# A macaron layer on one core: shorter filler, one expert's weights on another queue, transposes of the mixed tiles moved

## The reference

```python
x = x + 0.5 * ffn(layernorm(x))
x = x + ssm(layernorm(x))
x = x + 0.5 * ffn(layernorm(x))

def ffn(x):     # 8 experts, top 2 of 8 by sigmoid scores; 2 shared experts
    scores = sigmoid(x @ w_router.T)
    comb = top-2 of scores, divided by their sum
    out  = sum_e comb[:, e] * (silu(x @ wg[e].T) * (x @ wu[e].T)) @ wd[e].T   # inner width 640
    out += sum_j (silu(x @ sg[j].T) * (x @ su[j].T)) @ sd[j].T
def ssm(x):     # selective scan over time, 16 states
    dt = softplus(xproj[:, :256]); B, C = the other 2 x 16 columns of xproj
    h = exp(dt * A) * h + dt * B * x;  y = (h * C).sum(states) + D * x
```

## Time and profile before

| | |
|---|---|
| median of 3 runs | 547.87 us (546.45, 547.87, 549.91) |
| the profiled execution | 546.11 us, of which its span 544.2 |
| TensorE busy | 522.5 us, 96% of the span |
| VectorE busy | 327.8 us |
| GpSimd busy | 230.5 us |
| ScalarE busy | 156.9 us |
| DMA | 67.72 MB, mean 124 GB/s |

### The profile page before, as it was taken

One profiled execution on the slowest core, in us unless ns is written; L12 is line 12 of the kernel. 1 busy time (PEld: TensorE's weight loads), 2 busy tenths in 40 slices (PEclk: granted clock), 3 DMA queues, 4 the chain that ended last, 5 costly groups with the idle time before them and its releaser, 6 DMA issues.

```text
span 544.2 us, 11101 instructions
## 1 busy us (share of the span) xinstructions
PE 522.5 (96%) x4386; PEld 422.4 (78%) x4387; DVE 327.8 (60%) x654; ACT 156.9 (29%) x336; POOL 230.5 (42%) x208
## 2 busy tenths in 40 slices
PE   8999999999979999999979999999997999999996
PEld 7998997458958888447979788964487999954695
DVE  3843526422555999997686399999768232522224
ACT  1111122221117445443202643554421011222210
POOL 1041100322303999995453189999700540000031
PEclk9999999999999999999989999999999999999999
DMA  7986993912204445540321436556100230210012
GB/s 225 398 322 227 394 381 133 316 60 59 70 11 130 114 136 144 152 118 25 105 68 69 118 101 121 133 145 154 34 21 2 98 88 29 78 40 13 20 55 74
DMA packets 41991, 67.72 MB, mean 124 GB/s; under 512 B 5041, under 2 KB 24753, under 8 KB 41937
## 3 DMA queue, kind: packets, MB, share of 16 engines
q1 hardware_dynamic: 29968, 40.75, 25.7%
q10 hardware_dynamic: 8400, 16.12, 8.0%
q0 software_dynamic: 3568, 10.10, 5.5%
HBM read 48.74 MB, written 18.22 MB: 123 GB/s over the span
## 4 chain that ended last, share of the span: by engine, by line
PE 53%; DVE 15%; POOL 14%; issue 10%; DMA 4%; ACT 2%; POOLq 0%; SPq 0%; DVEq 0%; ACTq 0%
PE ps L513 18%; PE ps L528 10%; PE ps L538 10%; POOL region L954 7%; PE ps L551 6%; POOL xnt L968 5%; DVE ps L1035 3%; DMA xg_rows<-region,pos 2%; PE ps L661 2%; PE ps L562 2%; DVE hb L990 2%; PE ps L713 1%; PE ps L683 1%; DMA region<-yg_rows,ypos 1%; PE ps L557 1%
## 5 line engine op out<-in xcount | busy, mean ns | idle before, releaser
L513 PEld LDWEIGHTS ps<-xt,w_gu 128*128 128x128 f32 x1360 | 156.3, 192 | 13.7 <-ACT xt L770 5.6
L513 PE MATMUL ps<-xt,w_gu 128*128 128x128 f32 x1360 | 161.3, 277 | 4.5 <-DVE xres L1005 2.8
L990 DVE SCALAR_TENSOR_TENSOR hb<-hb,ps 128x640 f32<-128x640 f32 x68 | 55.5, 816 | 134.3 <-ACT hb L752 134.0
L538 PE MATMUL ps<-w_dn,hb 128*128 128x256 f32 x520 | 122.1, 383 | 0.0
L538 PEld LDWEIGHTS ps<-w_dn,hb 128*128 128x128 f32 x520 | 96.0, 193 | 11.2
L752 ACT ACTIVATE hb<-ps 128x640 f32<-128x640 f32 x68 | 47.4, 698 | 173.6 <-PE ps L513 167.2
L513 PE MATMUL ps<-xnt,w_gu 128*128 128x128 f32 x720 | 86.3, 279 | 5.5 <-DVE xres L1005 5.5
L513 PEld LDWEIGHTS ps<-xnt,w_gu 128*128 128x128 f32 x720 | 84.8, 195 | 7.5 <-DVE xres L1005 5.9
L968 POOL TENSOR_TENSOR xnt<-xnt,hh 128x512 f32<-128x512 f32 x64 | 81.8, 1278 | 1.3 <-DVE hh L1040 1.3
L935 POOL DMA_INDIRECT region<-yg_rows,ypos x32 | 30.6, 955 | 116.4 <-DMA yg_rows<-ob 94.8
L1035 DVE TENSOR_TENSOR_SCAN ps<-ps,region 128x512 f32<-128x512 f32 x64 | 78.2, 1223 | 0.9 <-POOL region L954 0.7
(11 more groups left out here) (104 smaller groups left out, 329.7 us busy)
## 6 DMA issues: line engine op xcount, KB each, us to landing
bcb<-bc_rows SPq DMA_DIRECT2D x22, 512.0 KB, 5.0
region<-bc_rows SPq DMA_DIRECT2D x10, 512.0 KB, 5.3
xg<-xg_rows SPq DMA_DIRECT2D x34, 128.0 KB, 3.6
w_gu<-in_wg ACTq DMA_DIRECT2D x6, 640.0 KB, 7.1
w_gu<-in_wu ACTq DMA_DIRECT2D x6, 640.0 KB, 8.5
w_dn<-in_wd ACTq DMA_DIRECT2D x6, 640.0 KB, 9.2
yg_rows<-ob SPq DMA_DIRECT2D x20, 128.0 KB, 4.1
xg_rows<-bcb SPq DMA_DIRECT2D x1, 2176.0 KB, 15.2
```

Of the source, the lines that this page charges most:

```text
L513: last = nc.tensor.matmul(gup(p)[:, c * P:(c + 1) * P], w_gu4[:, e, k, c * P:(c + 1) * P], x, start=(k == 0), stop=(k == KC - 1))
L538: ins = nc.tensor.matmul(outp(p), hb[:, p, c * P:(c + 1) * P], w_dn4[:, e, c, :], start=(c == 0), stop=(c == IC - 1))
L990: nc.vector.scalar_tensor_tensor(out=h, in0=h, scalar=1.0, in1=gup(p)[:, 0:I], op0=ALU.add, op1=ALU.mult).then_inc(s_a, 1)
```

## The change

FILL goes from 15 to 10. Expert 1 leaves EARLY and is issued by ScalarE behind tile 3, ahead of expert 2. In `first(n)`, gate and up of the next tile are issued in three pieces where there were two: column blocks 0 to 3, then (for a mixed tile n) the transposes of n's hidden rows and of the rows of tile n+2, then blocks 4 to 7 with the signal for tanh, then blocks 8 and 9. For a shared or whole tile n nothing stands between the pieces.

```diff
--- before.py
+++ after.py
@@ -35,7 +35,7 @@
 OVER_CLEARED = (ROWS - OVER_ROW) // P
 STEPS = 16
 
-FILL = 15
+FILL = 10
 
 
 
@@ -350,8 +350,8 @@
         N_SC = 2 * TT * 16
 
 
-        EARLY = (E + 1, 0, 1)
-        LATE = {3: (2,), 4: (3, 4), 5: (5,), 6: (6,), 7: (7,)}
+        EARLY = (E + 1, 0)
+        LATE = {3: (1, 2), 4: (3, 4), 5: (5,), 6: (6,), 7: (7,)}
 
         def weights_of(e):
 
@@ -596,11 +596,13 @@
                     if loaded(n + 1):
                         pe.wait_ge(s_xtc, turned(n + 1))
                     free[n + 1] = free_expert(segment(n + 1), index_of(n + 1)) if kind_of(n + 1) == "mixed" else None
-                    gate_up(n + 1, free[n + 1], 0, 8).then_inc(s_gate, 1)
+                    gate_up(n + 1, free[n + 1], 0, 4)
                 if kind_of(n) == "mixed":
                     pe.wait_ge(s_h, n + 1)
                     turn_hidden(hb[:, q, :], hidden_turned(q)).then_inc(s_tr6, 1)
                     rows_of(n)
+                if n + 1 < TILES:
+                    gate_up(n + 1, free[n + 1], 4, 8).then_inc(s_gate, 1)
                 rest_of_gate_up(n + 1)
 
             def second(n):
```

## The result

The changed kernel takes **542.74 us** (median of 22 runs, 539.08 to 545.71). The kernel before, run beside it on the same chip, takes 547.81 us (22 runs, 543.32 to 550.05). The ratio is 0.9915 with a 95% interval of 0.9894 to 0.9936: a gain of 0.85%. I had said 546.3 us in a range of 543.5 to 549.3. The profiled execution took 544.18 us against 546.1 before. So this pair of executions shows only 2 of the 5 us.

A forecast was written before the change was run, and what follows sets the result against it. TensorE, busy 522.5 of 544.2 us, was taken as the bound. Terms -1.5 (filler), -0.9 (weights) and +0.8 (mixed tiles) sum to -1.6 us: 546.3 us against the median 547.87, range 543.5 to 549.3.

The forecast's parts named there:

- The weights: At the row load near 49 us: expert 1's later loads free the scatters and end TensorE's wait, gain 0.9 us.
- the second scatters: Second group of four scatters on GpSimd: forecast to issue from about 34 us instead of 38.84.
- The mixed tiles: Transposes moved ahead in mixed tiles: forecast as a net cost of 0.8 us, bounds a gain of 1.7 to a loss of 2.5.
- worth nothing by itself: Mixed tiles: with unchanged counts on a bound TensorE, the moved transposes bring no gain and only move two waits.
- The new wait: First mixed tile of each scan: TensorE waits 1.2 us for VectorE's product; down products start 0.35 us later.
- The filler: Head of the program: ten passes of zeros fewer, filler over at 9.0 us, router products at 12.7; gain 1.5 us.
- the head gives nothing: Rival, head: the clock falls in the longer thin stretch or the filler already ended near the rows; 547.8 us, chance 0.2.
- the thin stretch: Head, between filler and tile 0: 9.0 to 12.7 us, TensorE idle only in pieces under 0.6 us, no clock fall.
- My own bound: Head: with the clock's rise as early as 5 us, the filler of 15 ends near 9.9; gain shrinks to about 0.2.
- The rule of the Trainium skill: Head: activity releases the throttled clock, idleness brings it back; less filler is a risk, sum 1.5 us higher.
- a shift of all that follows: Everything after the head waits on TensorE, directly or through the routing, so the head's saving moves all later work equally.
- The rival by which both slow stretches of the earlier trace stay fast: Rival, later slow-clock stretches, one from 280.5 us: both stay fast, 2 x 1.5 us more; 543.3 us, chance 0.07.

The follow-up runs named there:

- e6: Unchanged copy of the changed kernel, for a second profile; 541.43 us, ratio 0.9925 to the kernel before.
- e5: Unchanged copy of the kernel before, for a second profile; 545.42 us, ratio 0.9986 to the kernel before.
- g1: Changed kernel with expert 1's weights back in their old place, SyncE's burst; 547.04 us, ratio 0.9966 to the kernel before.
- g4: Unchanged copy of the changed kernel, run beside the leave-one-out versions; 545.14 us, ratio 0.9918 to the kernel before.
- e3: Kernel before with only the transposes of the mixed tiles moved; 546.52 us, ratio 0.9956 to the kernel before.
- g2: Changed kernel with the mixed tiles' transposes back behind eight column blocks; 549.4 us, ratio 0.9995 to the kernel before.
- e8: Changed kernel with the transposes of each scan's first mixed tile left in their old place; 541.9 us, ratio 0.9917 to the kernel before.
- e1: Kernel before with only FILL lowered from 15 to 10; 547.53 us, ratio 0.9973 to the kernel before.
- h1_short5: Changed kernel with five 8-column products added behind the ten filler products; 547.35 us, ratio 0.9967 to the kernel before.
- h4_fill20: Changed kernel with 20 filler products instead of 10; 548.11 us, ratio 0.9996 to the kernel before.
- i1_before: Unchanged copy of the kernel before, for a third trace; 549.76 us, ratio 0.9982 to the kernel before.

## Why the prediction was wrong

**The weights: right at their place.** Forecast -0.9; at the row load the traces show -1.07 (after), -1.0 (e6 against e5). Left out of the whole change they cost 1.9 us in the timed runs (g1 against g4), of which the larger part can be the wait that an earlier head would meet (1.3 us in g1). The times were off: the second scatters went out at 36.33, not 34, with the slow clock in front. And I had not seen that on four of the chips the moved weights also hold ScalarE near 103 us, which costs over 2 us where the transposes keep their old place.

**The mixed tiles: the step that failed.** I charged 0.8 us; they gain about 1.5 in the traces, and in the timed runs 2.8 alone (e3) and 4.3 within the change (g4 against g2, which includes the ScalarE hold). I had called the move worth nothing by itself, since the counts are unchanged, and two parts of the step were wrong. I took the earlier trace rows as the whole of TensorE's waiting for the copy. That view lists only gaps that are left between modelled ends, and ten of the other fourteen mixed tiles had their down products right behind the copy as well and hid about 0.1 us each. And I charged the later down products, 0.35 us at a scan's first mixed tile. The new wait was as forecast (1.17 against 1.2), but the down products lost 0.16, not 0.35: from the end of VectorE's product (225.78) to their start are 3.57 us, where I had added up 3.8 from rounded terms. And a later part of the same move I had not costed at all. Behind the last mixed tile of the scan stands VectorE's addition to the residual rows, with which the next segment's norm begins. In the timeline before:

```profile
255.81 1.28 DVE L1203 TENSOR_TENSOR xres<-xres,ps 128x512 f32<-128x512 f32 x2
```

and after:

```profile
253.66 1.28 DVE L1205 TENSOR_TENSOR xres<-xres,ps 128x512 f32<-128x512 f32 x2
```

It starts 2.15 us earlier, where TensorE's shift was 1.54: ScalarE's tanh of the next tile, for which VectorE waits before it, no longer stands behind the copy and starts at 251.34 instead of 253.48. So TensorE's next tile starts 0.59 us earlier. From tile 30's down products to tile 31's are 7.96 us in all fourteen traces with the moved transposes and 8.5 in all six without.

**The filler: not kept in the head.** The 1.5 us exist (e8: -1.58), but in seven traces of eight the slow clock takes them back. The timed runs give the filler 1.8 us alone (e1) and 1.5 to 3 us within the change, near my 1.5, and that is luck: in e1's trace the head gives nothing and the boundary at 150 us gives 1.6. This was my rival "the head gives nothing", which I had given 0.2. I had argued from the earlier trace rows that a fall needs a long standstill, and from the earlier trace rows that the thin stretch would have none. My own bound said otherwise: with an early rise the filler ends near 8, the rows are ready at 9.4, and TensorE stands 1.4 us. I had worked out that case for the filler of fifteen, where it only shrinks the gain, and not for ten. The rule of the Trainium skill that I had weighed (TensorE: Matmul & The Clock Gate, Part 1), that idleness brings the slow clock back, pointed the right way. The traces agree in part: seven falls came behind 0.7 to 1.4 us of standing, and three, with thirteen products or more, behind none.

**What was missing.** The boundary at 150 us, -1.6 us in the first pair of traces and -0.1 from e5 to e6. My remark that everything later is "a shift of all that follows" excluded it.

**The sum again**, from the traces: head 0 (the mean over eight traces; +1.7 in the first), row load -1.05, mixed tiles -1.5, boundary -1.6 with a long landing before, together about -4.2. The timed differences are 5.1, 4.9 and 4.2 us (the result, e6, g4). Of these four numbers the first three are shown in traces that agree with one another; the last is seen but not explained, and with e5's landing the sum is only -2.7. So about 2.5 of the 5.1 us have no shown cause. The rival by which both slow stretches of the earlier trace rows stay fast did not come about in the first pair: over 279.5 to 283 and 420 to 424 us the granted clock is 0.69 and 0.80 after, and 0.61 and 0.57 before. Half of it did in e6_after and e8_scanfirst, where the first stretch keeps the full clock (e6 over 279.5 to 283: 1.00), which is 1.3 us.

## What to carry to other kernels

A wait that a full engine's queue hides can be read from the distance of equal steps and from the end of the operation it waits for, and not from the list of its gaps: where a copy ends within 0.2 us of the products that need it, moving it earlier can pay at every repetition. Filler that keeps a clock up runs at two speeds, and in the execution in which it runs fastest it may end before the work behind it is ready; here that went with a fall of the clock in most executions, and where the filler reached the work the fall was rarer (three traces of ten), not absent. Two parts of a change can also depend on each other, so each is worth timing alone and left out. And one profile of each kernel is one draw: here the two first ones showed 1.9 of 5.1 us, and copies of both kernels show which steps repeat.

## What the runs showed that I had not expected

- TensorE's clock fell behind a stretch in which it stood only 0.7 to 1.4 us and otherwise ran transposes and 8-column products (seven traces of eight); in h1_short5 even 0.27 us of standing, behind ten narrow passes, went ahead of a fall at 12.3 us. A fall lasted 3.4 or 6.8 us, 1.7 or 3.3 us lost. With thirteen, fifteen and twenty products one trace each fell with no standing before it.
- The landing of the same four gathers took one of two values: the fifth issue follows the fourth by 3.5 to 3.8 us or by 5.0 to 5.4 us, with one trace between (4.5, h4_fill20).
- Two copies of one program on different chips (before and i1_before) differ by pauses of 2.2 us in the same three tiles, which the waits view puts down to "issue" or to ScalarE's copy.
- Moving one expert's loads to ScalarE's queue goes with a hold of ScalarE near 103 us, nearly 60 us behind their issue, in ten traces of ten on four chips and in none of the four traces with the loads in their old place there.
